# Metaformer block on one core: two filters per convolution matmul, and one block of gathered pixels weighed earlier

## The reference, cut to what matters

```python
# 1. deformable 3x3 convolution
offset = conv2d(ln_c(x), offset_w) + offset_b           # 18 channels
mask   = sigmoid(conv2d(ln_c(x), mask_w) + mask_b)      # 9 channels
val    = mask * bilinear_gather(ln_c(x), base + offset) # 9 taps x 4 corners
x      = x + silu(batchnorm(einsum(val, weight)))
# 2. spectral mixer over the 1024 pixels as a sequence t
u      = ln_t(tokens(x))
for branch i, frac in enumerate((1, 2, 4, 8)):          # only the first T/frac tokens
    out_i = sum over 16 filters k: causal_conv(phi[:, k], u) * sigma_k**0.25 @ M[i, k]
            + 3-tap autoregressive part with M_u[i]
x      = x + from_tokens(sum_i w_i * out_i)             # w: hard softmax weights
```

## Time and profile before

| what | value |
|---|---|
| median of 3 runs | 757.17 us (754.53 to 760.55) |
| the profiled execution: its own time | 751.24 us |
| its span | 749.4 us |
| mean granted TensorE clock over the span | 0.784 |
| PE busy, matmul / weight load | 506.5 us / 376.8 us |
| DVE, ACT, POOL busy | 314.9, 179.7, 292.7 us |

### The profile page before, as it was taken

The page is one execution under the profiler, slowest core; times in us unless marked ns, Lnnn a source line. Parts: engine busy times, 40 slices in busy tenths (PEclk is TensorE's granted clock), DMA queues, the critical chain, the costliest instruction groups (busy, mean ns, idle before and its releaser), DMA issues.

```text
span 749.4 us, 13126 instructions
## 1 busy us (share of the span) xinstructions
PE 506.5 (68%) x5598; PEld 376.8 (50%) x5598; DVE 314.9 (42%) x800; ACT 179.7 (24%) x421; POOL 292.7 (39%) x295
## 2 busy tenths in 40 slices
PE   5976429246208845785889549891168648999998
PEld 3443105135106613564678329771156327788997
DVE  6467411868602703850438007187009025753000
ACT  1121012113004302321232102240033113334322
POOL 1257750634770372556253732237702745000000
PEclk9966558659557966986999759996569759899999
DMA  8526373811330131222121320113300321000000
GB/s 166 127 79 158 101 204 117 282 56 50 98 105 2 46 107 45 66 71 85 44 64 37 100 64 23 44 44 98 98 21 30 105 64 56 16 2 3 9 2 9
DMA packets 43778, 54.27 MB, mean 72 GB/s; under 512 B 24664, under 2 KB 34142, under 8 KB 43721
## 3 DMA queue, kind: packets, MB, share of 16 engines
q0 software_dynamic: 13824, 37.77, 17.1%
q1 hardware_dynamic: 23841, 13.42, 6.9%
q10 hardware_dynamic: 6056, 2.26, 1.3%
HBM read 50.12 MB, written 3.30 MB: 71 GB/s over the span
## 4 chain that ended last, share of the span: by engine, by line
PE 55%; another core or an unknown queue 25%; issue 10%; DVE 5%; ACT 4%; DMA 1%; SPq 0%; ACTq 0%; DVEq 0%
PE bank L888 30%; PE bank L900 7%; PE bank L760 2%; PE bank L834 2%; PE bank L824 2%; ACT u_conv L661 2%; PE bank L793 2%; PE bank L741 1%; PE bank L795 1%; PE bank L732 1%; PE bank L845 1%; PE bank L919 1%; ACT vT L628 1%; DMA filt<-in_L_ffn_phi_dram 1%
## 5 line engine op out<-in xcount | busy, mean ns | idle before, releaser
L269 POOL DMA_INDIRECT G<-corner_table,idx x288 | 290.0, 1007 | 343.9 <-DVE idx L362 155.2
L888 PE MATMUL bank<-filt,u_hi 128*64 128x256 f16 x2560 | 255.3, 291 | 135.1 <-issue 85.6
L888 PEld LDWEIGHTS bank<-filt,u_hi 128*64 128x64 f16 x2560 | 152.8, 114 | 172.0 <-issue 112.0
L888 PE MATMUL bank<-filt,u_lo 128*64 128x256 f16 x1280 | 198.9, 291 | 15.1 <-issue 15.1
L661 ACT ACTIVATE u_conv<-bank,f_scale 128x256 f32<-128x256 f32 x256 | 118.6, 474 | 303.8 <-PE bank L888 153.6
L900 PE MATMUL bank<-u_conv,mixw 128*64 128x256 f32 (+1 forms) x640 | 94.2, 377 | 9.9 <-issue 9.2
L888 PEld LDWEIGHTS bank<-filt,u_lo 128*64 128x64 f16 x1280 | 84.3, 117 | 24.6 <-issue 22.4
L455 DVE TENSOR_TENSOR G<-G,bank 128x2304 f32<-128x2304 f32 x32 | 81.5, 2548 | 0.3
L467 DVE TENSOR_SCALAR expo<-expo 128x128 f32<-128x128 f32 x16 | 3.6, 227 | 183.1 <-ACT expo L638 172.1
L459 DVE TENSOR_TENSOR V<-G 128x576 f32<-128x576 f32 x32 | 24.3, 758 | 110.0 <-PE bank L825 73.4
L900 PEld LDWEIGHTS bank<-u_conv,mixw 128*64 128x64 f32 x640 | 47.9, 155 | 20.5 <-issue 18.9
(11 more groups left out here) (158 smaller groups left out, 387.3 us busy)
## 6 DMA issues: line engine op xcount, KB each, us to landing
filt<-filter_rows SPq DMA_DIRECT2D x16, 514.0 KB, 9.1
G<-corner_table,idx POOLq DMA_INDIRECT x288
corner_table<-n_uT SPq DMA_DIRECT2D x12, 128.0 KB, 2.9
mixw<-in_x_dram SPq DMA_DIRECT2D x2, 512.0 KB, 6.0
filt<-in_L_ffn_M_phi_plus_dram SPq DMA_DIRECT2D x8, 128.0 KB, 4.9
out_dram<-o_sb ACTq DMA_DIRECT2D x8, 128.0 KB
filt<-n_L_ffn_M_phi_minus_dram ACTq DMA_DIRECT2D x4, 128.0 KB, 4.0
corner_table<-n_uT ACTq DMA_DIRECT2D x4, 128.0 KB, 3.3
```

Source lines behind the costliest of these rows:

```text
L269: pool.indirect_dma_start(G[:, k, tap, :], None, corners[bp], bass.IndirectOffsetOnAxis(ap=idx[:, q % 2, k, tap:tap + 1], axis=0)).then_in ...
L888: last = pe.matmul(conv_ps[b2][C * src:C * src + C, 0:2 * P].rearrange("c (p a) -> c p a", p=2), u[:, NJ * bp + j2, b2, src], h, start=(j2 ...
```

## The change

Six things change. (1) `convolve` takes a pair g of filters, 2g and 2g+1: each matmul streams 512 columns (filter, parity, position) in place of 256, into the whole bank, so there are half as many matmuls and weight loads for the same columns. It is called at even k only. (2) `copy_products(n, g)` has two activations for each image, of the same size as before. (3) `u_conv` doubles, to hold two pairs; `w_diag`, used only in the set-up, becomes a view of its memory. (4) `mix` runs two filters behind: `mix(k-2)` at each k from 2, and `mix(14)`, `mix(15)` at the end of the pass. (5) PE waits at k = 3 for `out_copied`, since the tokens go to a bank from which ACT copies the last pass's output. (6) DVE runs `weigh(q,1,1)` ahead of `finish(q,0)` for q from 1.

```diff
-        w_diag = sb("w_diag", [P, BRANCHES, 3, P])
-        u_conv = sb("u_conv", [P, 2, 2, 2, P])
+        u_conv = sb("u_conv", [P, 2, 2, 2, 2, P])
+        w_diag = u_conv[:].rearrange("s g k b p a -> s (g k b p a)")[:, 0:BRANCHES * 3 * P].rearrange("s (r v d) -> s r v d", r=BRANCHES, v=3)
...
                 weigh(q, 1, 0)
+                weigh(q, 1, 1)
                 finish(q, 0)
-                weigh(q, 1, 1)
...
-            def copy_products(n, k):
+            def copy_products(n, g):
                 for b2 in range(2):
-                    act.wait_ge(conv_done[b2], K * n + k + 1)
-                    act.activation(u_conv[:, k % 2, b2], conv_ps[b2][:, 0:2 * P].rearrange("c (p a) -> c p a", p=2), ACT.Copy,
-                                   scale=f_scale[:, k:k + 1]).then_inc(conv_copied[b2], 1)
+                    act.wait_ge(conv_done[b2], K // 2 * n + g + 1)
+                    for k in range(2):
+                        act.activation(u_conv[:, g % 2, k, b2], conv_ps[b2][:, 2 * P * k:2 * P * k + 2 * P].rearrange("c (p a) -> c p a", p=2),
+                                       ACT.Copy, scale=f_scale[:, 2 * g + k:2 * g + k + 1]).then_inc(conv_copied[b2], 1)
...
                 for k in range(K):
-                    copy_products(n, k)
+                    if k % 2 == 0:
+                        copy_products(n, k // 2)
...
                     for b2 in range(2):
-                        pe.wait_ge(conv_copied[b2], START + K * n + k)
+                        pe.wait_ge(conv_copied[b2], START + K * n + 2 * g)
...
-                                    h = filt_h[:, k, src, part, lag + 2 - src:lag + 2 - src + P]
-                                    h = bass.AP(h.tensor, h.offset, [h.ap[0], [(1, -1)[src] * 2 * HLEN + src, 2], [1, P]])
-                                    last = pe.matmul(conv_ps[b2][C * src:C * src + C, 0:2 * P].rearrange("c (p a) -> c p a", p=2),
+                                    h = filt_h[:, 2 * g, src, part, lag + 2 - src:lag + 2 - src + P]
+                                    h = bass.AP(h.tensor, h.offset, [h.ap[0], [4 * HLEN, 2], [(1, -1)[src] * 2 * HLEN + src, 2], [1, P]])
+                                    last = pe.matmul(conv_ps[b2][C * src:C * src + C, :].rearrange("c (k p a) -> c k p a", k=2, p=2),
...
                 for k in range(K):
-                    convolve(k)
+                    if k % 2 == 0:
+                        convolve(k // 2)
                     if k == ODD_TOKENS_AT:
+                        if n:
+                            pe.wait_ge(out_copied, n)
                         turn_tokens(2 * n + 1)
-                    if k:
-                        mix(k - 1)
+                    if k >= 2:
+                        mix(k - 2)
...
+                mix(K - 2)
                 mix(K - 1).then_inc(pass_mixed, 1)
```

More of the change, by code:

```diff
@@ L872, in _, with convolve @@
                           for s in range(seg0, seg0 + nseg)]
-                def convolve(k):
+                def convolve(g):
                     if n == 0:
-                        pe.wait_ge(filt_loaded[k], 16)
+                        for k in range(2 * g, 2 * g + 2):
+                            pe.wait_ge(filt_loaded[k], 16)
                     for b2 in range(2):
-                        pe.wait_ge(conv_copied[b2], START + K * n + k)
+                        pe.wait_ge(conv_copied[b2], START + K * n + 2 * g)
                         for j2 in range(j + 1):
-                            if k == 0 and b2 == 0 and j2 == j:
+                            if g == 0 and b2 == 0 and j2 == j:
                                 pe.wait_ge(u_ready, 2 * n + 2)
@@ L900, in mix @@
                             last = pe.matmul(acc[C * p:C * p + C, 0:2 * P].rearrange("e (b a) -> e b a", b=2)[:, :, a0:a1],
-                                             mixw[:, s, p, C * k:C * k + C], u_conv[:, k % 2, :, p, a0:a1],
+                                             mixw[:, s, p, C * k:C * k + C], u_conv[:, k // 2 % 2, k % 2, :, p, a0:a1],
                                              start=False, stop=False, skip_group_check=True)
```

## The result

The kernel after took 724.31 us, the median of 4 runs (718.49 to 725.11); the kernel before, in the same comparison, 755.85 (747.45 to 760.55). The ratio is 0.960 with a 95% interval of 0.950 to 0.970. The profiled execution took 725.11 us, its span is 723.3 us, and its mean granted clock 0.787. On another chip it came again as 724.06 us, ratio 0.952 (0.942 to 0.963). Ratios with an interval compare only the faster executions of each kernel, so they are not always the quotient of the medians; on one further chip (the kernel before at 773.1 us) only one of its seven executions, at 753.18 us, was a faster one, so the ratios from there are quotients of medians, without an interval, and against 753.18 they would be 0.02 to 0.03 higher.

What follows compares the result with a forecast made beforehand. Gathers that starve PE of instruction starts, alternating with PE work while POOL idles, were taken as the bound. Terms -19.6 - 1.3 - 1.0 = -22 us took the profiled 751.24 to 729, or 735 from the 757.17 median; range 700 to 768.

Steps and rivals of the forecast that it cites:

- Part 1: 512-column matmuls in the last two passes, without gathers: 672 pairs become 336, saving 1.3 us (bounds 0 and 8).
- the rest: Mixing two behind removes a wait for ACT at the last two pass ends, 1.0 us; the other edits, 0.
- Part 2: Inside gathers, halved convolution instructions let more filters finish; together with Part 3, -19.6 us over six stretches.
- free budget of 234 (j = 0) or 265: PE instructions at full pace from a gather's start, before the starved pace of 2.2 to 4.0 per us.
- -16 and -105: Budget left at j = 2 and 3 once 283 and 372 instructions have turned the first row's result.
- Part 3: DVE weighs the fourth block first: gather in one go of 47.1 us, starved stretch 11 to 12 us longer.
- (12 - done)c + 2c + 3.7: From t = 50 us to `finish`: filters not done plus two, at c = 1.10 to 3.09 us each, plus 3.7.
- A: Inside gathers, the full pace is limited by time, ending at 10 to 11 us: +20, net 755; chance 0.14.
- B: First row's exponential stays behind the gather's end, delaying `finish` and the second row; together with A, 768; chance 0.14.
- C: Inside gathers, ACT's late starts set the pace, not PE's instruction count: within 5 us, 757; chance 0.10.
- D: PE hardly starved in gathers: both j = 0 cycles 10 us shorter, four others 8 each: 683; chance 0.12.

Runs made afterwards that it cites:

- order_only: The kernel before with only DVE's order changed, weigh(q,1,1) ahead of finish(q,0): 769.55 us, ratio 1.011 to the kernel before.

## Why the prediction was right or wrong

**The sign and most of the size** were right: 735 forecast, 724.31 measured, so -31.5 us in the medians; in the profiled execution -26.1 us against -22. A part of the closeness is luck: the stretches from gather to gather gained 28.2 us against 19.6, and a head that was 4.6 us longer, mostly or all spread, took some of it back.

**Part 1** held. PE's timeline at the higher clock, in the last pass but one (j = 2):

```profile
643.09 0.62 PE L891 MATMUL bank<-filt,u_hi 128*64 128x512 f16 x4
...
647.02 1.05 PE L903 MATMUL bank<-u_conv,mixw 128*64 128x256 f32 x8
```

Between them lie six rounds of three pairs: 3.93 us / 18 = 218 ns, the 2 x 107 + 4 that the earlier trace rows gave. With "the rest" the end of the kernel gained 2.5 us (2.6 in the other execution), against 2.3 forecast. The new wait on `out_copied` was not tried by itself.

**Part 2** had the mechanism right and its sizes wrong. The twin kernel with 256 columns shows that the number of instructions brings the gain, and neither the grouping nor the copies. But the step "With a free budget of 234 (j = 0) or 265, and afterwards 2.2 (j = 0), 2.7 (j = 1) and 4.0 per us (j = 2, 3)" took averages of one kernel for constants. The budget came out at 308 to 372. That a PE which starts fewer instructions per us uses it up later fits this (21.5 to 24.9 per us before, 16.6 to 18.6 after), but was not tried apart; the pace behind it was 1.8 (j = 0), 3.0 (j = 1) and 1.3 (j = 3), and falls from block to block. The two errors partly cancel: the cycles came out as 70.3, 80.5 and 87.5 us for j = 1, 2, 3, against 72.1, 79.7 and 89.9. (In the working, -16 and -105 belong to a budget of 267 and not 265; it changes less than 0.1 filter.)

**Part 3 had the wrong sign, and this is the step that failed.** The sentence was "part 3 takes back much of it": nine gathers more in one go, priced as a cost, and nothing bought with them but the start of POOL. By itself the edit does cost (1.011). What the sum left out is who else waits for the row's last block: PE's `turn_values` of the second row, at k = 11. I let it start only when twelve filters were done, behind the gather; with pairs and the new order PE gets to it 19 us in at j = 0. Of the stretch (12 - done)c + 2c + 3.7 a part then lies inside the gather: the second row's `finish` began 53.9 us after the gather's start (234.97 - 181.05), not 57.1, and the j = 0 cycles ended at 67.2 and 67.7 us instead of 70.4. In the profiled spans the order is worth -15.2 us when the pairs are there; the kernels were not timed beside one another.

**The rivals.** A (a budget of time) falls: the onset was at 12 us or less and is now between 16.6 and 21. B (the first row's exponential behind the gather) falls for the kernel after, at 8.2 and 16.4 us; `order_only` shows it at j = 3 (57.1 us into a gather of 46.5), with the cycle at 98.8. C (instructions do not count) falls by the twin with 256 columns. D (hardly starved) did not happen by this change; the pauses came nearer to it, and from 724.06 to 591.35 us they are worth far more than the 52 us it was priced at.

**What is still open** is the cause of the decay. It is not bytes, not packets in proportion, not code. It comes with uninterrupted runs of indirect DMAs from POOL, PE and ACT both start late in it, and 2.5 us of pause take much of it away. Whether it is the number of these DMAs, or something that POOL does for each, no run shows. One rival of the theory could not be parted from it: every run here, the timed ones too, comes with its clock and span, so was recorded. The Trainium skill's "NOTIFIC — the notification-queue block", section "Overflow: three behaviours, one of which stalls the engine", says that the block which writes such records holds its producers back rather than lose one inside. A limit in number of instructions and not in bytes could look like that. Recording alone does not do it: in the last two passes, without a gather, PE starts 908 instructions in 50 us (640 to 690) at a granted clock of 1.00, 18 per us, and its pace holds. But no run here was without the recorder, so whether an unrecorded execution starves as much beside the gathers is not shown, nor how much of 0.774 it would keep.

## What to carry to other kernels

When an engine's instruction rate collapses beside a long run of DMAs issued from POOL, and neither bytes nor code explain it, count its instructions per block of DMAs; if they decay, try a wait for each block to land before the next is issued. Here a pause of 2.5 us in 14 made the gathers 14% longer and took the kernel from 724.06 to 591.35 us, 18% less. And when a step is moved on one engine, list everyone who waits for what it makes, and where they will be when the other edits are in: the same moved line cost 1.1% alone and, by the profiled spans, gained 2% with the pairs.

## What the runs showed of the hardware that was not expected

PE's matmuls and weight loads beside back-to-back indirect DMAs went from 254 to 106, 26 and 9 per block of nine (11 to 13 us each) with 1024 bytes a row; with 512 it was 254, 80, 29 and 10. A gap of 0.8 us between blocks in place of 0.3 changed the counts little (256, 122, 34, 13), one of 2.46 us much (38 rising to 170). Under the same gathers the granted clock follows the starved engine down, from 1.00 to 0.50, so that part of what the pauses give back is clock: its mean over the span went from 0.787 to 0.879 in the fastest version.
